# One 128-node window per tile in a four-layer graph network: half the one-hot products, duplicates on VectorE, degrees in the attention loop

## The reference

```python
# 0: relations
hw = einsum('nd,rdf->rnf', h, weight_r)             # 8 relations
M = segment_sum(hw[etype, src] / deg[dst][:, None], dst)
x0 = relu(0.2 * h + 0.8 * M)
# 1: attention
e = tanh(concat(h[src], h[dst]) @ W_attn.T + b_attn) @ w_out
ex = exp(e - segment_max(e, dst)[dst])
z = segment_sum((ex / segment_sum(ex, dst)[dst])[:, None] * h[src], dst)
# 2: gated Chebyshev convolution, K = 3, state zero
deg = segment_sum(edge_weight, src); dis = 1 / sqrt(deg)
w = -dis[src] * edge_weight * dis[dst]              # Tx1 = P x, Tx2 = 2 P Tx1 - x
# 3: graph convolution
out = segment_sum(edge_weight[:, None] * (x @ weight)[src], dst) + bias
```

## Time and profile before

| | |
|---|---|
| median of 3 runs | 2012.38 us (2007.74 to 2017.11) |
| the profiled execution: its span (the profile gives no other time of it) | 2533.2 us |
| chain that ended last, by engine | another core or an unknown queue 28%, PE 26%, issue 20%, DVE 14%, POOL 5%, DMA 4% |
| DMA | 272.07 MB, mean 107 GB/s |

### The profile page before, as it was taken

How to read it: one execution, slowest core, us unless ns; L and a number is a source line. 1 busy time by engine, 2 the same in 40 slices (tenths; PEclk the granted TensorE clock), 3 DMA queues, 4 the chain that set the end, 5 groups by cost and what they waited for, 6 DMA issues and landing times.

```text
span 2533.2 us, 28723 instructions
## 1 busy us (share of the span) xinstructions
PE 1374.4 (54%) x7844; PEld 1089.7 (43%) x7845; DVE 991.2 (39%) x2889; ACT 200.8 (8%) x390; POOL 1235.7 (49%) x1381
## 2 busy tenths in 40 slices
PE   4455555565621556566555651111111898879877
PEld 2455554554511456556555640000000898434423
DVE  7555554554604333334333440000000676300488
ACT  2000000000000111111111100000000111000200
POOL 1666666666672366565666677677777000000000
PEclk8766767677755555555555555555555898899989
DMA  5444343435200222222222200000000002988878
GB/s 165 150 155 153 120 152 118 150 121 168 65 1 0 68 63 66 65 62 64 66 66 64 66 21 0 0 0 1 0 0 0 0 0 103 353 335 353 326 295 336
DMA packets 154645, 272.07 MB, mean 107 GB/s; under 512 B 44030, under 2 KB 100154, under 8 KB 151546
## 3 DMA queue, kind: packets, MB, share of 16 engines
q1 hardware_dynamic: 111322, 229.57, 24.9%
q0 software_dynamic: 40064, 41.32, 6.6%
q10 hardware_dynamic: 3232, 0.82, 0.1%
HBM read 215.32 MB, written 56.29 MB: 107 GB/s over the span
## 4 chain that ended last, share of the span: by engine, by line
another core or an unknown queue 28%; PE 26%; issue 20%; DVE 14%; POOL 5%; DMA 4%; DVEq 1%; ACT 1%; SPq 1%; POOLq 0%; ACTq 0%
PE acc L987 10%; PE acc L1035 7%; POOL rings L736 5%; PE acc L1029 4%; DVE rings L1367 2%; DVE big L1826 2%; DMA big<-pairs_by_src 2%; DVE rings L1401 2%; DVE rings L1402 1%; DVE big L1391 1%; DMA rings<-local_rows 1%; PE acc L1009 1%; DMA relation_rows<-big 1%; DMA rings<-relation_rows,idx_ring 1%
## 5 line engine op out<-in xcount | busy, mean ns | idle before, releaser
L987 PE MATMUL acc<-rings 128*65 128x128 f32 x3328 | 576.1, 326 | 634.4 <-issue 459.6
L987 PEld LDWEIGHTS acc<-rings 128*65 128x65 f32 x3328 | 456.0, 168 | 709.4 <-issue 694.3
L736 POOL DMA_INDIRECT rings<-relation_rows,idx_ring x416 | 409.5, 984 | 281.9 <-issue 184.1
L736 POOL DMA_INDIRECT rings<-attention_rows,idx_ring x416 | 394.6, 948 | 305.1 <-issue 234.3
L1029 PE MATMUL acc<-attend_mem,rings 128*128 x1664 | 373.8, 411 | 266.2 <-issue 182.3
L1029 PEld LDWEIGHTS acc<-attend_mem,rings 128*128 128x128 f32 x1664 | 367.3, 328 | 273.0 <-issue 273.0
L753 POOL DMA_INDIRECT pairs_by_src<-fed_val,fed_idx x416 | 405.6, 975 | 149.4 <-issue 120.0
L1425 DVE TENSOR_SCALAR rings<-iota_bf,col_local,score 128x256 f32<-128x256 bf16 x416 | 139.4, 408 | 480.3 <-remote 371.8
L786 POOL DMA_INDIRECT big<-support_rows,ext_node x4 | 3.9, 963 | 450.6 <-DMA support_rows<-big 449.7
L1680 DVE TENSOR_TENSOR rings<-acc,rings 128x512 f32<-128x512 f32 x52 | 35.6, 684 | 352.0 <-remote 343.9
L1035 PE MATMUL acc<-big,attend_mem 128*64 128x512 f32 x700 | 163.0, 600 | 9.1 <-DMA big<-pairs_by_src 9.1
(11 more groups left out here) (279 smaller groups left out, 895.0 us busy)
## 6 DMA issues: line engine op xcount, KB each, us to landing
big<-pairs_by_src SPq DMA_DIRECT2D x54, 2048.0 KB, 12.5
pairs_by_src<-zeros SPq DMA_DIRECT2D x24, 1792.0 KB
big<-key_rows SPq DMA_DIRECT2D x52, 512.0 KB
rings<-local_rows SPq DMA_DIRECT2D x52, 256.0 KB
big<-pairs_by_src SPq DMA_DIRECT2D x12, 1024.0 KB, 12.3
rings<-relation_rows,idx_ring POOLq DMA_INDIRECT x416
pairs_by_src<-fed_val,fed_idx POOLq DMA_INDIRECT x416
rings<-attention_rows,idx_ring POOLq DMA_INDIRECT x416
```

The costliest lines, as they stand in the source:

```text
L736: pool.indirect_dma_start(ring[h][:, u, 0:width], None, table, bass.IndirectOffsetOnAxis(ap=idx_ring[h][:, u:u + 1], axis=0),).then_inc(ga ...
L987: m = pe.matmul(node_sums[:, bass.ds(at[u] * P + w * P, P)], rows[h][:, u, :], onehot[h][:, u, w * P:(w + 1) * P], start=False, stop=False ...
```

## The change

**Windows.** A tile of 128 sorted edges is taken to span at most 128 nodes from its first destination on. The sums are made over that one window, so each tile has one product of 128 columns instead of two, in both `add_up` loops. The windows start at any node, so the sums lie in eight banks that overlap by 128 nodes; `sum_at` holds each tile's column, worked out in the preparation, and `turn_nodes` adds the two parts of a block that lies in two banks (32 products instead of 25). The one-hots of eight tiles are made by one tensor_tensor over 1024 elements, with both operands repeated. In the weighted sums the weight moves from the one-hot to the rows: eight small activations per half-step in place of one copy.

**Duplicates.** PE's products of keys go. DVE compares eight tiles' keys in one operation, multiplies with the edges' weights, and sums over each tile. The weights come through the same broadcast as the keys, which becomes 1 MB instead of 512 KB per half-step; `key_rows` is stored in two parts. Each duplicate then holds the same sum and the same address, so `indices`, the dump area and a dozen small operations on constants go.

**Degrees.** Their one-hots and products move to the attention loop, and the small operations on them from the transition to behind the weighted sums' one-hots.

**Look-up.** One product per tile gives the rows of both blocks (128 columns), with the weights loaded once, into two banks per half-step; copy_predicated then picks the upper row where a flag says so. ACT copies the flags. The transposed one-hot is over 128 instead of 256 partitions' worth, in one operation.

The number of gathers and scatters, and their places in POOL's list, stay. The diff, cut to its core:

```diff
-        key_rows = nc.dram_tensor("key_rows", [TC * P, P], F32).ap()
+        key_rows = nc.dram_tensor("key_rows", [TC * P, 2 * P], F32).ap()
...
-            sp.dma_start(key_rows.rearrange("(c t) p -> t c p", t=P), row_key).then_inc(keys_stored, 16)
+            for part, r in ((0, row_key), (1, raw_weight)):
+                sp.dma_start(key_rows.rearrange("(c t) (k p) -> t c k p", t=P, p=P)[:, :, part, :], r).then_inc(keys_stored, 16)
...
-                        act.activation(rows[h][:, :, :], edge_rows[:, bass.ds(it * (2 * H) + h * H, H), :], ACT.Copy
-                                       ).then_inc(rows_copied, 1)
+                        for u in range(H):
+                            t = bass.ds(it * (2 * H) + (h * H + u), 1)
+                            o = act.activation(rows[h][:, u, :], edge_rows[:, t, :].rearrange("p a c -> p (a c)"), ACT.Copy,
+                                               scale=weight_e[:, t])
+                        o.then_inc(rows_weighted, 1)
...
                         for u in range(H):
-                            for w in range(2):
-                                m = pe.matmul(node_sums[:, bass.ds(at[u] * P + w * P, P)], rows[h][:, u, :],
-                                              onehot[h][:, u, w * P:(w + 1) * P],
-                                              start=False, stop=False, skip_group_check=True)
...
+                            m = pe.matmul(node_sums[:, bass.ds(at[u], P)], rows[h][:, u, :], onehot[h][:, u, :],
+                                          start=False, stop=False, skip_group_check=True)
...
-                            for w in range(2):
-                                m = pe.matmul(work[2 + h][:, u * D:(u + 1) * D], onehot_t[h][:, w, u * P:(u + 1) * P],
-                                              there[:, w * D:(w + 1) * D], start=(w == 0), stop=False, skip_group_check=True)
+                            m = pe.matmul(found[h][:, u * 2 * D:(u + 1) * 2 * D], onehot_t[h][:, u * P:(u + 1) * P], there,
+                                          start=True, stop=True, skip_group_check=True)
                         m.then_inc(slot_free[key], 1)
+                        pe.wait_ge(degree_hots_ready, it * 2 + h + 1)
+                        for u in range(H):
+                            m = pe.matmul(degree_bank[:, 0:3 * NB], onehot_lo[h][:, u, :], hi_parts[h][:, u, :],
+                                          start=False, stop=False, skip_group_check=True)
+                        m.then_inc(degrees_added, 1)
...
+            def window_hots(h, cols):
+
+                return dve.tensor_tensor(onehot[h], iota_bf[:, 0:P].unsqueeze(1).to_broadcast([P, H, P]),
+                                         col_window[:, cols].unsqueeze(2).to_broadcast([P, H, P]), ALU.is_equal)
...
+                dve.tensor_tensor(onehot_lo[h], iota_bf[:, 0:P].unsqueeze(1).to_broadcast([P, H, P]),
+                                  col_lo[:, cols].unsqueeze(2).to_broadcast([P, H, P]), ALU.is_equal)
...
+                        dve.tensor_tensor(eq[h], key_ring[h][:, :, 0:P], col_key[:, cols].unsqueeze(2).to_broadcast([P, H, P]),
+                                          ALU.is_equal).then_inc(eq_ready, 1)
+                        dve.wait_ge(rows_free["rel"], it * 4 + 2 * h + 2)
+                        window_hots(h, cols).then_inc(onehot_ready["rel"], 1)
+                        dve.wait_ge(eq_ready, it * 2 + h + 1)
+                        dve.tensor_tensor(eq[h], eq[h], key_ring[h][:, :, P:2 * P], ALU.mult).then_inc(keys_read, 1)
+                        dve.wait_ge(keys_read, it * 2 + h + 3)
+                        dve.tensor_reduce(dup_val[:, cols], eq[h], AX.X, ALU.add).then_inc(dups_ready, 1)
...
-            dve.tensor_copy(local_bf[:, :, :], row_local[:, :, :]).then_inc(rows_derived, 1)
+            then(dve.tensor_single_scalar(row_upper, row_window, float(P), ALU.is_ge))
+            then(dve.scalar_tensor_tensor(local_bf[:, :, :], row_upper, float(-P), row_window, ALU.mult, ALU.add))
+            dve.sem_inc(rows_derived, 1)
+            then(dve.tensor_single_scalar(window_first[:, :, :], raw_dst[:, :, 0:1], float(TOP), ALU.min))
+            dve.tensor_tensor(row_window, raw_dst[:, :, :], window_first[:, :, :].to_broadcast([P, TC, P]), ALU.subtract)
...
+                    dve.copy_predicated(both[:, :, 0], upper_ring[h][:, :].unsqueeze(2).to_broadcast([P, H, D]), both[:, :, 1]
+                                        ).then_inc(picked, 1)
+                    dve.wait_ge(picked, it * 2 + h + 1)
+                    dve.tensor_tensor(msg[h][:, :, :], both[:, :, 0], rows2[h][:, :, 0:D], ALU.add).then_inc(bank_read, 1)
```

More of the change, by code:

```diff
@@ L56, in gnn_kernel @@
     VB = N // P
+    SPAN = BANK - P
+    TOP = VB * P
+    SUM_BANKS = 8
+    assert SUM_BANKS * SPAN == TOP and SPAN % P == 0 and NODES == TOP + P
+    PER_SPAN = SPAN // P
     SLOTS = 6
@@ L242, in gnn_kernel @@
         stat = [sb(f"stat{i}", [P, NB, 1]) for i in range(6)]
+        degree = sb("degree", [P, NB, 1])
         dis = sb("dis", [P, NB, 1])
@@ L967, in clear_sums @@
                     pe.wait_ge(wait, 2)
-                for i in range(MAIN + 1):
+                for i in range(SUM_BANKS):
+                    if key == "agg" and i == SUM_BANKS - 1:
+                        pe.wait_ge(expo_ready, 1)
                     m = clear(banks[i])
-                    if i >= MAIN - 1:
+                    if key == "agg" and i >= SUM_BANKS - 2:
                         m.then_inc(slot_free[key], 1)
@@ L1015, in look_up @@
                 for h in range(2):
-                    pe.matmul(work[2 + h][:, :], zeros[:, 0:P], zeros[:, :], start=True, stop=True
-                              ).then_inc(slot_free[key], 1)
+                    for i in range(2):
+                        m = pe.matmul(found[h][:, i * BANK:(i + 1) * BANK], zeros[:, 0:P], zeros[:, :], start=True, stop=True)
+                    m.then_inc(slot_free[key], 1)
+                clear(degree_bank).then_inc(degrees_added, 2)
                 with pe.Fori(0, IT) as it:
```

333 lines of the change are left out of this document (143 added, 190 removed).

## The result

The changed kernel takes 2117.31 us in the median of 4 runs (2108.91 to 2129.14), the kernel before 2012.08 (4 runs): a ratio of 1.052, 95% interval 1.049 to 1.055. The change is slower, as forecast (2095, range 1960 to 2150). Its profiled execution, the longest of the four, took 2129.14 us with a span of 2127.3. The first line is the page's busy times after, the next three are POOL's groups over the whole span, and the last is its first gather; they answer to the earlier trace rows.

What follows compares the result with a forecast made beforehand. POOL's indirect transfers were taken as the bound from 59 us to the end of the scatters. 2012 + 2.7 (start) + 125 (holds) - 15 (relation gathers) = 2125, less 30 for waits: 2095 us, range 1960 to 2150.

Steps and rivals of the forecast that it cites:

- a thing of the profile: PE's slow stretches during POOL's indirect transfers, taken as absent from the runs; the profiled execution was 521 us longer.
- rival 3: PE's slow stretches during scatters are partly real in the runs, so halved PE work pays: about 1920 us; chance 0.06.
- The 70 us not in POOL's sum: Whole kernel: POOL's list summed to 1942, 70 us short of the median; POOL's own waits and time around the span.
- the 30: Deduction of 30 us from those 70, as a shorter PE step and a late POOL shrink waits for rows.
- the forecast's own range: Times if new DVE operations hold POOL: 2010 to 2170 us, most of it 2040 to 2150; chance 0.60.
- The start: Before the first gather: longer DVE chain to the keys and a second key store, +2.7 us, bounds 0 and 6.
- The holds: DVE operations with two SBUF inputs delay POOL transfers 0.48 us on average: relation 75, attention 25, sums 25; together 125 us.
- rival 2: Holds exist but are short because POOL and DVE fall into step: a third of 125, giving 2012 us; chance 0.12.
- The -15: Relation gathers: their mean of 984 against attention's 948 ns goes with L1402, which leaves that loop, saving 15 us.
- Rival 1: The new DVE operations, with repeated operands, don't hold POOL: 1940 to 1980, about 1965 us; chance 0.22.
- The inferred sentence: Skill page: tensor_tensor takes only the read interface, descriptor generation needs the write one; by that the 125 us are nothing.

Runs made afterwards that it cites:

- e_before_2: The kernel before, unchanged, timed and profiled again in a later job: 2013.83 us, profiled span 2017.2.
- e_best: Changed kernel with two-SBUF-input operations cut in four, the degrees' low one-hots' places in PSUM and padding spread: 2027.84 us, ratio 1.0096 to the kernel before.
- e_split: Changed kernel with each 1024-element operation with two SBUF inputs cut into four of 256: 2048.78 us, ratio 1.018 to the kernel before.
- e_att_psum_2: Changed kernel with the row of places for the degrees' low one-hots read from PSUM: 2067.23 us, ratio 1.030 to the kernel before.
- e_best8: Changed kernel, padding spread, degrees' places in PSUM, other two-SBUF-input operations cut in eight, attention's transposed one-hots in four: 2064.48 us, ratio 1.027 to the kernel before.
- e_before: The kernel before, unchanged, in a job where all its runs were long (2509 to 2552 us in two such jobs): 2542.75 us, span 2540.9.

## Why the prediction was right, and where its steps were off

**What bounds the kernel.** Right for the timed runs: POOL's idle time is nearly the same before and after, and PE's busy time fell from 1263.0 us (e_before_2) to 929.2 without a gain (in the three loops by 329, where I had about 400). But the reasoning was wrong in a step: "If the runs had them too they would take 2533, so I take them for a thing of the profile." The slow stretches of PE were no thing of the profile. Other timed runs of the same kernel take 2509 to 2552 with them, and there rival 3 holds and the ratio is 0.9455. The forecast stands on the record's times being of the other condition, which the prediction could not know from one profile.

**The 70 us not in POOL's sum.** I called them waits for rows that a shorter PE step would shrink, and took 30 off. e_before_2 shows them: relation stage 552.8 against my 534 (19: 8 by gathers of 1004 ns where I had 984, the rest pauses), early scatters 91.5 against 83 (8, the transition's operations beside them), attention 525 against 519, late scatters 486 against 458 (28: 11 by scatters of 1007 ns in place of 976, 10 by POOL's feed copies, which take 19 where I had 9, and 8 by pauses), tail 300 against 289. Of all this 7.6 us wait for PE's L987. The change gave none of it back: the idle time before POOL's transfers stayed. So the 30 was a term without a ground in the rows. Without the deduction the forecast was 2125; the run is 2117. (The lower end of the forecast's own range, 2010, should by its terms be 1995.)

**The start.** Forecast +2.7, the first gather at about 61.5; it stands at 61.32, 1.9 later than in e_before_2.

**The holds.** The mechanism was right, and its sum nearly. Between the two profiles POOL's transfers are 94 us longer (416 x 12 ns in the relation stage = 5, 416 x 122 in attention = 51, 352 x 112 in the late scatters = 39, and 1 less in the early ones), against 125 - 15 = 110 forecast. Their places were mis-sized: the means forecast as 1120, 1010 and 1040 ns (relation gathers, attention gathers, late scatters) came out as 1016, 1067 and 1119.

- Relation stage, forecast 75 - 15 = 60, measured 0 in the stage's length and 5 in the mean. Against the 945 ns of e_before_2's attention gathers the new gathers (1016) are 30 us longer in all, where I had 75, and the old ones (1004) were 25 longer, where I had 15. In the new kernel L1384, L1415, a reduction (L1417) and L1410 stand in a row, and it is mostly the first that holds: 33 gathers are held to the end of L1384, 10 to that of L1415 and 3 to that of L1410. POOL's timeline, then the vector engine's, of the changed kernel:

```profile
66.51 1.06 POOL L740 DMA_INDIRECT rings<-relation_rows,idx_ring  x1 [0.30 <-issue]
67.88 1.97 POOL L740 DMA_INDIRECT rings<-relation_rows,idx_ring  x1 [0.30 <-issue]
70.15 0.95 POOL L740 DMA_INDIRECT rings<-relation_rows,idx_ring  x1 [0.30 <-issue]
71.40 0.95 POOL L740 DMA_INDIRECT rings<-relation_rows,idx_ring  x1 [0.30 <-issue]
...
66.68 1.22 DVE L1384 TENSOR_TENSOR rings<-iota_bf,col_window 128x1024 f32<-128x1024 bf16 x1
67.81 1.22 DVE L1415 TENSOR_TENSOR big<-big 128x1024 f32<-128x1024 f32 x1
...
69.16 1.22 DVE L1417 TENSOR_REDUCE dup_val<-big 128x1024 f32 x1
70.30 1.22 DVE L1410 TENSOR_TENSOR big<-big 128x1024 f32<-128x1024 f32 x1
```

  A held gather ends 0.82 after the operation and the next starts 0.30 later, 1.12 in all; the operations follow each other every 1.13 to 1.15 us (1.35 before L1417). So POOL, once held, starts each transfer as an operation ends, or just before one begins (70.15 against 70.30), and passes. Only 43 relation gathers took over 1.045 us, where an even spread over 156 operations would have held more than 100; in e_before_2 there are 113 such, if short ones. That was rival 2's mechanism ("POOL and DVE fall into step"), at work in this stage.
- Attention, forecast 25, measured 51. The one operation there comes behind others that wait for the gathers, so it too is in step with POOL, in the bad phase: 50 gathers begin inside it and are held by 0.79 us on average, 46 of them by some 0.86, where my even spread said 0.48 an operation. That is 40 us; the other 10 are the transposed one-hots, one SBUF input, which I had costed at nothing.
- Late scatters, forecast 25, measured 43: 44 of the 52 one-hot operations of the sums hold a scatter, by 0.88 us on average.
- The -15 was a term of the right sign, with its cause in part unread. Operations with one SBUF input (and a scalar per partition) hold too: of the 139 relation gathers of e_before_2 over 1.0 us, 117 ran beside L1401 and 112 beside L1402, and 79 of the 83 that began inside an L1401 with 0.13 us or more of it left were lengthened, by 0.13 us on average. One of them (start 284.07), POOL's timeline and then the vector engine's:

```profile
284.07 1.07 POOL L736 DMA_INDIRECT rings<-relation_rows,idx_ring  x1 [0.31 <-issue]
...
284.00 0.34 DVE L1401 TENSOR_SCALAR rings<-iota_bf,col_local 128x256 f32<-128x256 bf16 x1
```

**The tail.** 14 us in the last scatter's landing and what waits for it stood in no step. The dump area's removal was told in the change, and I costed only its instructions.

**How much was luck.** The forecast added 83 us to the time before, and 105 came. Its direction follows from the mechanism. That the number came so near is in part luck: the relation stage stood 55 us under its term, attention 26 and the late scatters 18 over theirs, the tail's 14 were in no term, and the 30 taken off for waits had no counterpart.

**Rivals.** Rival 1 is refuted: repeated operands and bf16 hold as a scan does. The inferred sentence of the Trainium skill, page "SBUF — State Buffer", section "Who interferes with whom", that tensor_tensor would not stall a DMA's descriptor generation, is not borne out for these indirect transfers (0.86 us with both inputs in SBUF, nothing with one in PSUM); the rule beside it, that two SBUF inputs contend with a GpSimd instruction that reads SBUF, is. Which part of a transfer is held, the reading of its addresses from SBUF or the writing of its descriptors, no run here tells. Rival 2 was at work in the relation stage, rival 3 in the long condition alone. What is left open is the 1% of e_best, 18 us.

## What to carry to other kernels

Before a stage is relieved, ask which engine's idle time would vanish; here the change cut PE's work by a quarter and paid with the one engine that had no idle time. Beside an engine that issues indirect DMAs all the time, an operand in PSUM or a cut into pieces of moderate size (256 elements here, not 128) was worth more than a shorter instruction list. And a spare area that looks like waste may be what keeps padding from writing one address 123 times.

## What the runs showed of the hardware

- A gather that starts inside one of the changed kernel's operations of 1024 elements with two SBUF inputs, 0.13 us or more before its end, ends 0.82 us after that operation, a scatter 0.84 or 0.85 after; only 4 gathers, which began within 0.02 us of an operation's start, were not held. With 24 operations of 128 elements back to back a gather can be held through the whole rest of the row (4.65 us); with operations of 256 elements (e_split) the relation gathers are held by 0.25 us at most.
- With one of the two inputs in PSUM, 50 of 50 such gathers were not held (e_att_psum_2).
- An operation of 1024 elements with one SBUF input in bf16, L1379, lengthens a gather too, even one that began before it: 41 gathers over 1.0 us end 0.12 or 0.13 us after it. Cut into four of 256 it does so hardly any more (mean 944 ns in e_best8). POOL's and the vector engine's timelines of the changed kernel, where the gather takes 0.36 us more than 0.95:

```profile
1010.87 1.31 POOL L740 DMA_INDIRECT rings<-attention_rows,idx_ring  x1 [0.30 <-issue]
...
1011.32 0.74 DVE L1379 TENSOR_SCALAR rings<-rings,iota_part 128x1024 f32<-128x1024 bf16 x1
```

- The last scatter, with 123 of 128 entries on one cell, takes 18.3 to 19.3 us to land in three traces, with dump cells of their own for them 7.40 in one, over 64 cells 2.2 to 2.4 in three.
- The same kernel on the same chip 9 took 2546 us in one job and 2009 in another. In the long condition other engines stand still for up to 80 us (87 in another place of e_before) while POOL issues scatters; what sets the condition is open.
